# Attention output stage: ScalarE casts the MLP's high part, VectorE forms x1's low part, images loaded in four pieces

## The reference, cut to what matters

```python
def _conv1x1(x, w, b):
    return jnp.einsum('bchw,oc->bohw', x, w) + b[None, :, None, None]
...
out = _conv1x1(out, proj_w, proj_b)
x1 = shortcut + out
h = _conv1x1(x1, c1_w, c1_b)
h = jax.nn.gelu(h, approximate=False)
h = _conv1x1(h, c2_w, c2_b)
return x1 + h
```

## Time and profile before

| | |
|---|---|
| median of 3 runs | 5248.26 us (5243.58 to 5248.89) |
| profiled execution, its time | 5249.56 us |
| profiled execution, its span | 5247.5 us |
| mean granted clock of PE | 0.953 |
| busy share of the span | PE 86%, DVE 83%, POOL 79%, ACT 59% |
| this stage: first weight load issued to last output | 2503.6 to 2722.0 us |
| first projection | 2522.6 us |

### The profile page before, as it was taken

How to read it: one execution, slowest core, us unless ns; L and a number is a source line. 1 busy time by engine, 2 the same in 40 slices (tenths; PEclk the granted TensorE clock), 3 DMA queues, 4 the chain that set the end, 5 groups by cost and what they waited for, 6 DMA issues and landing times. The chain is left out here.

```text
span 5247.5 us, 68516 instructions
## 1 busy us (share of the span) xinstructions
PE 4506.7 (86%) x15210; PEld 2090.3 (40%) x15210; DVE 4334.4 (83%) x3524; ACT 3121.4 (59%) x6582; POOL 4126.0 (79%) x1958
## 2 busy tenths in 40 slices
PE   7998897955999999992788888889898888989887
PEld 2332564621666666661442232222222233222322
DVE  4776545554289999999779999999999999999996
ACT  6886555532011111110238888888888888888886
POOL 2544555534288989889669999999999999999993
PEclk9999998987999999996899999999999999999998
DMA  2000101147677877782408888788888888888883
GB/s 54 1 1 10 53 28 48 37 133 227 140 142 137 149 142 149 145 148 27 103 18 202 200 199 201 193 198 199 204 202 194 200 200 200 203 200 201 202 200 97
DMA packets 385380, 733.14 MB, mean 140 GB/s; under 512 B 77948, under 2 KB 119080, under 8 KB 370920
## 3 DMA queue, kind: packets, MB, share of 16 engines
q1 hardware_dynamic: 385128, 730.30, 60.3%
HBM read 594.31 MB, written 82.32 MB: 129 GB/s over the span
## 5 line engine op out<-in xcount | busy, mean ns | idle before, releaser
L2213 POOL TENSOR_TENSOR l_hc<-l_h,l_c_rep 128x1024 f32<-128x1024 f32 x768 | 1799.2, 2377 | 18.5 <-DVE l_h L2284 15.7
L1400 POOL TENSOR_TENSOR l2b_prod<-l2b_v,l2b_attn 128x1568 f32<-128x1568 f32 x276 | 937.7, 3460 | 233.6 <-ACT l2b_attn L1361 118.1
L2284 DVE TENSOR_TENSOR_SCAN l_h<-l_p,l_h,l_bu 128x1024 f32<-128x1024 f32 x448 | 1027.5, 2334 | 5.8 <-ACT l_bu L2121 4.3
L1968 PE MATMUL l_p<-l_stacked,l_pick 96*128 96x512 f32 x1536 | 558.9, 445 | 216.2 <-DVE l_h L2284 204.7
L1448 DVE TENSOR_REDUCE l2b_osum<-l2b_prod 128x32 f32<-128x1568 f32 x384 | 665.7, 1781 | 63.2 <-POOL l2b_prod L1400 59.5
L2202 POOL TENSOR_TENSOR l_pool_bu<-l_du_rep,l_b_sb 128x1024 f32<-128x1024 f32 x256 | 609.3, 2380 | 40.3 <-DMA l_du_rep<-du_scratch 40.1
L2268 DVE TENSOR_TENSOR l_bu<-l_du_rep,l_p 128x1024 f32<-128x1024 f32 x512 | 614.1, 1199 | 25.7 <-DMA l_du_rep<-du_scratch 18.6
L1353 ACT ACTIVATE l2b_logits<-l2b_conv,l2b_this_b 98x512 f32<-98x512 f32 x96 | 66.1, 689 | 862.6 <-PE l2b_conv L1318 862.6
L1968 PEld LDWEIGHTS l_p<-l_stacked,l_pick 96*128 96x128 f32 x1536 | 242.1, 189 | 796.1 <-DVE l_h L2284 651.1
L1977 PE MATMUL l_p<-l_hc,l_y_pick 128*32 128x512 f32 x3072 | 524.0, 606 | 5.0 <-POOL l_hc L2213 4.9
L2284 DVE TENSOR_TENSOR_SCAN l_h<-l_p,l_h,l_pool_bu 128x1024 f32<-128x1024 f32 x224 | 524.8, 2343 | 1.1 <-ACT l_pool_bu L2121 1.0
(11 more groups left out here) (269 smaller groups left out, 9003.8 us busy)
## 6 DMA issues: line engine op xcount, KB each, us to landing
l_du_rep<-du_scratch SPq DMA_DIRECT2D x1536, 256.0 KB, 5.0
l2b_img_high<-qkv_scratch SPq DMA_DIRECT2D x192, 306.2 KB, 5.7
l2b_img_low<-qkv_scratch SPq DMA_DIRECT2D x192, 306.2 KB, 9.5
l_stacked<-l_parts SPq DMA_DIRECT2D x512, 96.0 KB, 3.3
l2b_v<-v_scratch SPq DMA_DIRECT2D x192, 152.0 KB, 6.6
qkv_scratch<-l2a_strip SPq DMA_DIRECT2D x32, 840.0 KB, 5.2
du_scratch<-l_du SPq DMA_DIRECT2D x128, 192.0 KB, 2.1
l_w_raw<-L_w_sed SPq DMA_DIRECT2D x32, 576.0 KB, 3.7
```

Of the source, the lines that this page charges most:

```text
L1400: return eng.tensor_tensor(dst.rearrange("q x (dy dx) -> q x dy dx", dx=WIN), window, attn_half[:, :, unit % 2].rearrange("q x (dy dx) -> ...
L1968: pe.matmul(p_da[p % 2][:, e, :], pick[:, GRP[i] % (Q // DL), :], stacked[:, par, GRP[i] * DL // Q, :], start=True, stop=True).then_inc(s_ ...
L2213: pool.tensor_tensor(hc[:, slot:slot + 2, :], h[:, 2 * p:2 * p + 2, :], c_rep[:, par, :].unsqueeze(1).to_broadcast([128, 2, N]), ALU.mult) ...
L2284: dve.tensor_tensor_scan(flat(h[:, 2 * p:2 * p + 2, :]), flat(p_da[p % 2]), flat(of), state, ALU.mult, ALU.add).then_inc(s_h, 1)
```

## The change

Four edits in `attention_out`:

1. The cast of h's high part moves from DVE to ACT. ACT's order in a step becomes gelu 0, gelu 1, cast 0, gelu 2, cast 1, cast 2. The wait for the c2 product of two tiles back moves with it.
2. The low part of x1 moves from POOL to DVE, straight behind the cast of x1's high part.
3. Each image is loaded in PIECES = 4 parts of 16 rows (two tiles): 16 pairs of DMAs in place of four, with a wait for each pair.
4. PE and DVE wait for a piece before every second tile, and no longer for an image before every eighth.

```diff
+    PIECES = PER_IMAGE // 2
+    ROWS_P = H // PIECES
...
-                    step(PER_IMAGE * b + j, j, True, True, True, b + 2 if j == PER_IMAGE - 2 else None,
+                    step(PER_IMAGE * b + j, j, True, True, True, PIECES * b + (j + 2) // 2 + 1 if j % 2 == 0 else None,
...
-                image = slice(b * HW, (b + 1) * HW)
-                sp.dma_start(o[:, b].rearrange("c h r x -> c h (r x)"), o_d[:, :, b]).then_inc(s_load, 16)
-                sp.dma_start(X[:, image], x_d[:, image]).then_inc(s_load, 16)
-                sp.wait_ge(s_load, 32 * (b + 1))
+                for piece in range(PIECES):
+                    at = b * HW + piece * (HW // PIECES)
+                    sp.dma_start(o[:, b, :, piece * ROWS_P:(piece + 1) * ROWS_P].rearrange("c h r x -> c h (r x)"),
+                                 o_d[:, :, b, piece * ROWS_P * XW:(piece + 1) * ROWS_P * XW]).then_inc(s_load, 16)
+                    sp.dma_start(X[:, at:at + HW // PIECES], x_d[:, at:at + HW // PIECES]).then_inc(s_load, 16)
+                    sp.wait_ge(s_load, 32 * (PIECES * b + piece + 1))
...
         def _(act):
+            def high(t, q, f):
+                act.wait_ge(s_h, FB * (t + 1) + f + 1 + H0)
+                act.activation(h_hl[0][:, 1 - q % 2, f, :], h[:, 1 - q % 2, f, :], ACT.Copy).then_inc(s_h_hi, 1)
...
                         act.activation(h[:, 1 - q % 2, f, :], p_h[f][:], ACT.Gelu, bias=c1_b[:, f:f + 1]).then_inc(s_h, 1)
+                        if f == 0:
+                            act.wait_ge(s_c2, t + C20)
+                        else:
+                            high(t, q, f - 1)
+                    high(t, q, FB - 1)
...
-                if mlp_in:
-                    dve.wait_ge(s_c2, t + C20)
-                    for f in range(FB):
-                        dve.wait_ge(s_h, FB * (t + 1) + f + 1 + H0)
-                        dve.tensor_copy(h_hl[0][:, 1 - par, f, :], h[:, 1 - par, f, :]).then_inc(s_h_hi, 1)
+                    dve.wait_ge(s_x1_hi, m + 1)
+                    dve.tensor_tensor(x1_hl[1][:, par, :], x1[:, keep, :], x1_hl[0][:, par, :], ALU.subtract).then_inc(s_x1_lo, 1)
...
-                if project:
-                    pool.wait_ge(s_x1_hi, t + 3)
-                    pool.tensor_tensor(x1_hl[1][:, par, :], x1[:, (q + 2) % KEEP, :], x1_hl[0][:, par, :], ALU.subtract).then_inc(s_x1_lo, 1)
```

More of the change, by code:

```diff
@@ L1547, in all_tiles @@
                 for j in range(PER_IMAGE):
-                    step(PER_IMAGE * b + j, j, True, True, True, b + 2 if j == PER_IMAGE - 2 else None,
+                    step(PER_IMAGE * b + j, j, True, True, True, PIECES * b + (j + 2) // 2 + 1 if j % 2 == 0 else None,
                          b + (j + 2) // PER_IMAGE)
             for j in range(PER_IMAGE):
-                step(T // N - PER_IMAGE + j, j, j < PER_IMAGE - 2, j < PER_IMAGE - 1, True, None, B - 1)
+                step(T // N - PER_IMAGE + j, j, j < PER_IMAGE - 2, j < PER_IMAGE - 1, True,
+                     PIECES * (B - 1) + (j + 2) // 2 + 1 if j % 2 == 0 else None, B - 1)
         @block.sync
```

## The result

The changed kernel takes 5211.34 us (median of 6 runs, 5209.67 to 5212.04), the kernel before 5248.88 (6 runs, 5243.58 to 5253.36). The ratio is 0.9924, with a 95% interval of 0.9914 to 0.9934: 0.76% faster, 37.5 us by the medians. The prediction was 5210 us, within 5203 to 5228.

A forecast was written before the change was run, and what follows sets the result against it. The prediction took PE (TensorE) as the bound after the change, at 5.00 us per tile. Pace 25.9, start 10.0, filling 0 and draining 2.9 sum to 38.8 us saved, giving 5209.5, rounded to 5210 us (range 5203 to 5228).

The forecast's parts named there:

- TensorE's need, 5.00 us: Matmuls of the stage: TensorE needs 5.00 us per tile and becomes the bound, with a period of 5.05 us, before 6.008.
- ScalarE: Casts of h moved to ACT: 0.64 us each, ACT working 3.99 us of 5.00 per tile, at no cost.
- What set the pace before: Steady part before the change: DVE and POOL hold each other off, 5.32 us of low parts plus 0.72 of pauses per period.
- The sum of those that exclude each other, 4.9 us: POOL's low parts 3.84, x1's cast 0.36, DVE's subtraction 0.69 us per tile; 4.2 if the subtraction doesn't exclude POOL.
- The pieces: Start of the stage: first quarter image lands 5.6 us after x's issue, saving 10.0 us (bounds 6.7 and 11.7).
- a first projection behind 2516: Sign that the forecast is wrong, at the stage's start; the first projection was expected at about 2512.6.
- Filling: First tiles of the stage: gain counted as 0 us, from -2 to +1.9, with a possible hold-up of some 3 us.
- Draining: Stage end: last output ends 14.4 us after the last projection's start, in place of 17.2, saving 2.9 us.
- A: Rival for the steady part: the DVE/POOL lock sets a period of 5.3 to 5.8 us; 5223 us, chance 0.20.
- B: Rival for the steady part: the subtraction misses POOL's pause every period, 7.4 us a period; 5273 us, chance 0.03.
- C: Rival for the steady part: the pace doesn't change and only the ends gain; 5235 us, chance 0.07.
- D: Rival for the start: pieces bring nothing, as a piece lands no sooner than an image; 5220 us, chance 0.02.

## Why the prediction was right

Term by term, predicted and measured in the profiled execution: the pace 25.9 us, measured 26.7; the start 10.0, measured 11.0; filling 0, measured 1.0; draining 2.9, measured 3.75; the sum 38.8, measured 42.45. The direction, the mechanism and the order of the terms hold. Every term was a little low. That the time came within 1.4 us of the 5210 forecast is partly luck: the stage gained 42.45 us and the medians only 37.5, and these 5 us, which lie within what the runs vary by, cancel most of what the sum lacked.

*TensorE's need, 5.00 us.* Right, and shown twice: the pace is 5.020 in each of the four kernels with both moves and all matmuls, and falls by the 0.69 us of three matmuls, in the short periods, when they are left out. It was read from the distances of matmuls. PE's busy time in the earlier trace rows, 37.61 of 40 us, would have given 5.65 us of a period of 6.008, since part of its standing still is counted there as busy. The pace term is low by 0.8 us only because I put 0.05 us on top of the 5.00 and the measured need is 5.02.

*ScalarE.* The cast was put at 0.64 us and took 0.625. The room was there. The prediction worked it out for the order with two GELUs ahead of the first cast; with each cast right behind its GELU the pace is the same. That the step between c1 and c2 is what hides the casts, and that 1.9 us per period would be lost without it, no run tested.

*What set the pace before.* That the pair of DVE and POOL sets the pace holds, and so does the reading that POOL pauses only where it lacks DVE's cast. Wrong was that DVE must wait for such a pause. I counted 0.36 us of POOL's time for x1's cast in the 4.9 us, and later expected 5.5 to 5.7 us of the casts alone on ACT. They gave 5.17, with no pause at all, and x1's cast got in. The pauses came from a circle: POOL kept out the very cast whose result it would need next.

*The sum of those that exclude each other, 4.9 us.* This step was too high: the next bound is 4.40. That DVE's subtraction and POOL keep each other off is what the runs show in kind (1.66 against 0.689 us). The Trainium skill's page "SBUF — State Buffer" says so too, in the section "SBUF: two separate sides", and has the lock held for the whole instruction. If the recorded durations were the time of the hold, they would add up to 4.85 us; the run gave 4.40. The measurement decides. What part of an instruction's recorded time is outside the hold was not measured apart.

*The pieces.* 5.6 us expected from x's issue to the release, 4.61 measured. The fixed part was too large: the image's 15.62 us and the piece's 4.61 lie on a line with 0.94 us at no bytes, while I had taken the 2.3 of a small load. That is the term's 1.0 us. In the other runs with pieces the first one took 4.75 to 5.21 us, by which the fixed part is at most 1.7 us, still under 2.3. One sign of being wrong that the prediction named did occur: a first projection behind 2516. It stands at 2517.23, but only because the stage began 5.63 us later in this execution (2509.26, not 2503.63). Counted from the stage's first DMA it came after 7.97 us, where the forecast of 2512.6 meant 9.0. The sign was set in absolute time, which a later start of the stage shifts; the term itself was too small, not too large.

*Filling.* I had set a possible hold-up of 3 us against a gain of 1.9. The subtraction of tile 2 was held for 1.0 us (the maximum of 1.667), and PE didn't wait for it there. Of the gain, 0.62 us came as foreseen: PE waits 0.31 us for the low part of tile 0, not 0.93. From tile 2's projection to tile 4's there were only 0.39 us more, 10.89 in place of 11.28, and not the 1.3 down to 10.0. TensorE's granted clock was 0.50 (its level of 1.2 GHz) from 2525 to 2526 and 1.00 (2.4 GHz) from 2527 to 2529; PE had been busy since 2517.23, but for a gap of 0.31 us. So tile 2's projection, at 2525.24, ran at the low level, and its period was 5.87 us where every later one is 5.02. The 10.0 had left this out.

*Draining.* 14.4 us expected from the last projection's start to the end, 13.49 measured. I had let tile 31's c1 stand behind one more projection, as in the steady part, with its first chunk done 6.55 us after tile 31's projection. But no tile follows tile 31, so that projection doesn't exist, and PE goes straight on to c1:

```profile
2676.69 0.40 PE L1572 MATMUL l2c_p_h<-l2c_x_high,l2c_w_c_high 96*128 96x512 f32 x1
...
2677.58 1.42 ACT L1619 ACTIVATE l2c_h<-l2c_p_h,l2c_c_b 128x512 f32<-128x512 f32 x2 [0.61 <-PE l2c_p_h L1574]
```

Its first GELU starts 5.91 us after the projection (2677.58 - 2671.67). The projection that I counted too much is 0.86 us, which accounts for the term's 0.85.

*Rivals.* A (the lock sets the pace): refuted, with 0.6 us between 5.02 and 4.40. It is near enough that it binds in every second period when TensorE loses three of its matmuls per tile. B (starvation): refuted, as the longest subtraction of all runs is 1.81 us, held for 1.1, which is less than one of POOL's low parts, even where POOL hardly pauses. C and D: refuted by the projections and by the pieces alone.

What stays open is why a cast before the change waited for two of POOL's instructions in a row (2.755 us) and with the pieces alone did so too (2.751), where in every other kernel of this study none waited for more than one. POOL's two stood end to end there, so a place to slip in, as in the run with the casts alone on ACT, was passed over.

## What to carry to other kernels

When two engines look full and one of them has instructions whose maximum is several times their median, add up what each needs at its minimum; moving the short instruction whose result the other waits for to a third engine took 0.84 us of 6.01 per tile here, though it is longer there (0.625 us against 0.414). Read what TensorE needs from the distances and ends of its matmuls, not from the idle column. In the fill and in the drain, count the work that is really there and at the clock granted there: here a projection that isn't there and the lower clock moved the two ends by some 0.9 us each. At the start of a stage, only the first tiles' data is worth waiting for: quarter loads brought some 11 us once, and nothing in the steady part.

## What the runs showed of the hardware

An instruction of VectorE that is held by GpSimd can get through between two GpSimd instructions that stand end to end, without a gap between them: with the casts alone on ScalarE, x1's cast did so in each steady period, held for 0.7 us, with GpSimd busy for 40.00 of 40 us. In the kernel before, a cast of h did not and was held through two (2.755 us). GpSimd's low parts grow beside such an instruction, from 1.29 to at most 1.73 us in the changed kernel. The durations that both engines' instructions have alone add up to more than the time they take together (4.85 against 4.40 us per tile, with two of the three c1 matmuls left out). ScalarE's cast of the same size is not held: 0.617 to 0.634 us with GpSimd busy throughout.

Small loads issued right behind a large one were late: the last weight, of 0.8 KB, landed 3.9 us after its issue behind a piece's two transfers of 384 KB each and the other weights, where 1.8 us was its time in the changed kernel:

```profile
l2c_cols<-L_cols_out SPq DMA_DIRECT2D x1, 0.8 KB, 1.8
```
